# Attention's layernorm statistics of x in head slot 5 instead of head slot 7

## What is computed

```
_layernorm(x) = (x - mean(x)) / sqrt(var(x) + 1e-5)
x = x + tanh(g_xattn[0]) * xattn(_layernorm(x), ctx_1024, Wq, Wk, Wv, Wo, bo)
x = x + tanh(g_ffn[0])  * ffn(_layernorm(x), router_w, w_gate, w_up, w_down, ws_gate, ws_up, ws_down)
```

## Time and profile before

| what | before |
|---|---|
| median of 3 runs | 1902.89 us (1900.71 to 1904.76) |
| the profiled execution | 1910.31 us, its span 1908.6 us |
| mean granted TensorE clock | 0.987 of full speed |
| TensorE (PE) busy | 1842.6 us, 97% |
| VectorE (DVE) busy | 1452.8 us, 76% |
| ScalarE (ACT) busy | 960.2 us, 50% |
| GpSimd (POOL) busy | 811.3 us, 43% |
| SyncE's DMAs | 216864 packets, 205.86 MB |

### The profile page before, as it was taken

One profiled execution on the slowest core, in us unless ns is written; L12 is line 12 of the kernel. 1 busy time (PEld: TensorE's weight loads), 2 busy tenths in 40 slices (PEclk: granted clock), 3 DMA queues, 4 the chain that ended last, 5 costly groups with the idle time before them and its releaser, 6 DMA issues.

```text
span 1908.6 us, 32817 instructions
## 1 busy us (share of the span) xinstructions
PE 1842.6 (97%) x11280; PEld 1556.7 (82%) x11280; DVE 1452.8 (76%) x3217; ACT 960.2 (50%) x2260; POOL 811.3 (43%) x1067
## 2 busy tenths in 40 slices
PE   6999999999997899999999999999999999999999
PEld 5889988998896778888878888877888887888887
DVE  5788888888775777777887777787777778867776
ACT  4777877787776643334443433353434334433332
POOL 3445555555445443424624343353333443333330
PEclk9999999999997899999999999999999999999999
DMA  7888898998886332121132212114122112311111
GB/s 219 172 189 191 190 197 191 201 207 190 193 197 160 84 112 84 45 78 45 55 115 73 66 56 76 46 40 149 47 75 78 47 54 71 118 44 67 45 45 45
DMA packets 217029, 207.96 MB, mean 109 GB/s; under 512 B 113824, under 2 KB 169120, under 8 KB 216864
## 3 DMA queue, kind: packets, MB, share of 16 engines
q1 hardware_dynamic: 216864, 205.86, 42.3%
HBM read 111.43 MB, written 18.87 MB: 68 GB/s over the span
## 4 chain that ended last, share of the span: by engine, by line
PE 74%; DVE 13%; issue 5%; POOL 3%; ACT 2%; DMA 1%; SPq 1%; DVEq 0%; POOLq 0%; ACTq 0%
PE gate_up L1297 31%; PE down L1811 18%; PE bank L797 16%; PE scores L900 2%; DVE ops_lo L1154 2%; DVE acc L1662 2%; PE probs_t L931 2%; POOL hidden L1510 1%; PE rows_t L787 1%; DVE x_in L651 1%; DVE probs L729 1%; PE y L924 1%; PE down L1790 1%; PE y L922 1%; ACT probs L607 1%
## 5 line engine op out<-in xcount | busy, mean ns | idle before, releaser
L1297 PE MATMUL gate_up<-xo_hi,ops_hi 128*128 128x512 f32 x1120 | 440.5, 393 | 13.4 <-DVE hidden L1273 4.5
L1297 PE MATMUL gate_up<-xo_hi,ops_lo 128*128 128x512 f32 x1120 | 436.6, 390 | 0.0
L1297 PE MATMUL gate_up<-xo_lo,ops_hi 128*128 128x512 f32 x1120 | 436.4, 390 | 0.0
L607 ACT ACTIVATE probs<-probs,neg_max 128x128 f32<-128x128 f32 (+1 forms) x512 | 229.3, 450 | 108.2 <-DVE neg_max L729 106.5
L1662 DVE SCALAR_TENSOR_TENSOR acc<-down,scale,acc 128x512 f32<-128x512 f32 x320 | 239.0, 748 | 35.1 <-PE down L1811 34.7
L1297 PEld LDWEIGHTS gate_up<-xo_hi,ops_hi 128*128 128x128 f32 x1120 | 210.6, 188 | 67.5 <-DVE gated L1273 9.6
L1811 PE MATMUL down<-d_hi,h_hi 128*128 128x512 f32 x640 | 249.0, 389 | 0.0
L1811 PE MATMUL down<-d_lo,h_hi 128*128 128x512 f32 x640 | 249.0, 389 | 0.0
L1811 PE MATMUL down<-d_hi,h_lo 128*128 128x512 f32 x640 | 249.0, 389 | 0.0
L1297 PEld LDWEIGHTS gate_up<-xo_lo,ops_hi 128*128 128x128 f32 x1120 | 210.5, 188 | 44.4
L1297 PEld LDWEIGHTS gate_up<-xo_hi,ops_lo 128*128 128x128 f32 x1120 | 210.6, 188 | 42.3
(11 more groups left out here) (183 smaller groups left out, 4423.3 us busy)
## 6 DMA issues: line engine op xcount, KB each, us to landing
g_raw<-in_w_gate SPq DMA_DIRECT2D x40, 512.0 KB, 3.8
u_raw<-in_w_up SPq DMA_DIRECT2D x40, 512.0 KB, 3.8
d_raw<-in_w_down SPq DMA_DIRECT2D x40, 512.0 KB, 3.7
k_stack<-k_hi SPq DMA_DIRECT2D x128, 128.0 KB, 2.5
q_stack<-q_hi SPq DMA_DIRECT2D x128, 128.0 KB, 2.5
c_in<-in_ctx_t SPq DMA_DIRECT2D x16, 512.0 KB, 4.4
x_in<-in_x SPq DMA_DIRECT2D x16, 512.0 KB, 5.3
k_stack<-k_lo SPq DMA_DIRECT2D x64, 128.0 KB, 2.6
```

The costliest lines, as they stand in the source:

```text
L607: ins = act.activation(p, p, ACT.Exp, bias=neg_max[:, s, t:t + 1], scale=-1.0, accum_out=row_sum[:, s, t:t + 1])
L1297: ins = pe.matmul(gu_ps[bank][:], ops[x][:, which, a, c, :], xo[y][:, b, c, :], start=(begins and c == 0 and i == 0), stop=(c == CH - 1 an ...
```

## The change

`LN_SLOT` is 5 and no longer 7. Both uses of the constant follow: VectorE's `statistics(ln)` and GpSimd's `inverse_std(ln)`. `X_LOAD`, `XN_SLOT` and all other numbers stay.

```
-    LN_SLOT, C_SLOT, XN_SLOT = 7, 12, 10
+    LN_SLOT, C_SLOT, XN_SLOT = 5, 12, 10
```

## The result

The changed kernel takes 1928.89 us in the median of 4 runs (1927.08 to 1934.21), the kernel before on the same chip 1901.8 us (1900.49 to 1904.76). The ratio is 1.0149, 95% interval 1.0131 to 1.0167: slower by 27 us. The profiled execution took 1934.21 us, its span 1932.5 us, at the same mean granted clock of 0.987 as before; against the profiled execution of before that is +23.9 us. The forecast was 1916 us with a range to 1927 us: the direction came true, the size did not.

What follows compares the result with a forecast made beforehand. The prediction took TensorE to bound attention, with SyncE's in-order queue the tightest resource beside it. Terms 0 + 1 + 13.0 + 0 - 0.9 = +13 us on 1903 us gave 1916 us, range 1902 to 1927 us.

Steps and rivals of the forecast that it cites:

- VectorE in a plain batch: Statistics in slot 5 delay slot 6's maximum, but TensorE needs it 2 us later; slot 10's wait swallows any gain: 0.
- The load of x_in: Landing 0.3 us before the statistics' new place, at slowest 0.8 us late: +1 us, bounds 0 and +6.
- It compounds: Rival, chance 0.10: late queue delays x1's store, x_res, then x_in and the statistics; 14 us more, 1930 us.
- GpSimd's order and the standstill: Newton and the additions precede head 6's split, so SyncE's queue stands still 3.1 us before head 6's turn.
- The load of hat rows: On SyncE's queue, 1.8 us later per batch; VectorE waits 2.6 us; net +13.0 us, bounds +5 and +21, or 0.
- The queue absorbs it: Rival, chance 0.24: gaps and long issues behind the standstill take most of it up; 1905 or 1907 us.
- The turned halves: Head 10's turn issues up to 3 us later, possibly late for TensorE's next batch: 0, bounds 0 and +4.
- The start: TensorE's 0.86 us wait for the first batch's second q_lo vanishes: -0.9 us, bounds -0.9 and 0.
- Faster: Rival, chance 0.06: time leaving slot 7 removes TensorE's slot 12 wait for t_lo, saving 9 us: 1894 us.

Runs made afterwards that it cites:

- e3: The changed kernel with SyncE's load of x_res issued in slot 4, behind the load of x_in, instead of slot 2: 1920.88 us, ratio 1.0072.
- e1: The changed kernel with GpSimd's Newton operations back in slot 7, VectorE's statistics staying in slot 5: 1930.68 us, ratio 1.0119.
- e2: The changed kernel with GpSimd's two additions to x_res in slot 8 instead of 6: 1907.71 us, against 1906.75 us for the kernel before.
- e8: The changed kernel with the statistics and Newton operations in slot 6 instead of 5, on both engines: 1944.59 us.
- e4: The changed kernel with the load of hat rows issued in slot 10 instead of 14: 1934.48 us.
- e7: The changed kernel with GpSimd's additions to x_res in slot 8 and the load of x_res in slot 4: 1901.18 us, ratio 0.9993.

## Why the prediction was wrong in size

**VectorE in a plain batch, 0.** Right for the changed kernel: with x_in on time (e3) the plain batches cost +1.1 us over five. But the cover that I named, TensorE's late need for slot 8, was not the whole of it. It also needs GpSimd to be idle beside the statistics. Where it is not (e1), the same move costs 23 us in slots 12 and 13, falls of the clock included. I had checked who waits for the group, not who runs beside it.

**The load of x_in, +1, bounds 0 and +6.** This is the step that failed. The waits grew by 16.5 - 6.2 = 10.3 us, and moving x_res behind x_in (e3) takes back some 15 us by the ratios, 10.7 us by the slots. I priced the load from its issue time of before, 305.90 us, and let only its landing vary. But the issue time itself moves: the queue that the same change makes late carries it. The rival *It compounds* had this chain link by link, with a chance of 0.10 and 14 us. e3 bears out its mechanism and its size, but not its place: it saw the price in the hat batches, and of the 10.7 us that e3 takes back in the slots 8.0 us lie in the five plain ones, and the waits begin in batch 2, before the first hat row. What I set against it, that TensorE is late too and gives the load its time back, does not prevent the loss: eight batches have such a wait, and only 1, 5, 7, 9 and 10 have none. A second part of the 10 us stands in no term of the sum, a fall of the clock behind a wait of 1.85 us in batch 12, which costs 1.5 us in slot 13.

**GpSimd's order and the standstill, 3.1 us.** Right: 2.75 us in batch 7, 4.5 us where x_in was late (136.57 us against the end of the issue before at 132.03 us, in batch 2). e2 shows it as the cause of both prices.

**The load of hat rows, net +13.0.** Mechanism right, size low: slots 2 and 4 cost +17.2 us. Two terms were off. The wait rose to 23.5 / 8 = 2.94 us a batch where I had 2.6, since the gaps behind the standstill gave nothing back. And of it TensorE paid more than I allowed: 17.1 us in the hat batches on top of the 1.9 us of before (the forecast had 1.8 us), 19.0 of 23.5 us, so 0.56 us a batch were free and not 0.75. Besides slot 4 a second place begins to pay, slot 2, where t_lo stands behind the moments; in the kernel before slot 2 took 2.64 to 2.65 us in every batch, whatever the wait. *The queue absorbs it*, which had 0.24, is out by the same rows: the way behind the turn kept its 17.05 us. Its condition, that the long issues vanish while the queue stands still, did not come true either: between 80 and 560 us there are 31 in the trace of before and 31 in that of the changed kernel.

**The turned halves, 0.** TensorE's waits for them rose from 8.4 to 9.9 us, 1.5 us, inside the bound of +4.

**The start, -0.9.** Right: -1.3 us until slot 0 of batch 1.

***Faster*, 0.06.** Its mechanism was real in part, and my ground against it was wrong. I held that VectorE has caught up in slot 10, so nothing arrives in slot 12. But a VectorE that comes to the pair L651 0.08 us earlier is through both halves before head 10's split can take hold between them: in batches 5, 7, 9 and 10 of the changed kernel slot 12 is 2.4 us and not 3.2 us. Over all batches the pair takes 3.9 us less than before, which batches with a late x_in overspent.

The sum, from the slots: hat rows +17.2; x_in +3.3 in slots 7 and 8, +5.8 of lateness in slot 12 and +1.5 from the clock, together +10.6; the shorter pairs -3.9; other slots +2.2. That is +26.1 us in batches 1 to 13, and with -1.3, -1.2 and +0.4 us outside them +24.0 us, against +23.9 us between the profiled executions and +27.1 us between the medians. The forecast had +13 for the first term, +1 for the second, and neither the third nor the fourth.

The Trainium skill's rule on refills of instructions ("Runtime: NRT & Kernel Launch", section "Instruction fetch mechanics"), which the prediction weighed and called mostly hidden, has rows after all. The transfers of the profile's instruction queue go with SyncE's long issues (248 of 294, as counted above). In batch 7 of the changed kernel the two turns beside such a transfer took 0.9 and 1.1 us longer than the usual 1.25 us. If the refill is the cause, which was not tested, it is not hidden on this queue.

**Not settled.** Four more kernels gave no result: the kernel before profiled again; the changed kernel with one Newton step in place of three (the dose of GpSimd's work between the splits); the changed kernel with both loads moved together; and the kernel before with L651 in slot 11. So how the loss grows with what stands between the splits rests on two points (e2 and the changed kernel) and on e8. That slot 12 follows the pair and its start is a rule that fits all ten traces, not the result of moving L651 alone.

## What to carry to other kernels

When a group moves to an earlier place on one engine, read what the engine that consumes it puts between two hand-overs to an in-order queue; whatever is needed soonest behind the queue pays for that distance, and moving one load forward moved the bill here (e4) and did not pay it. Price a load from the issue time that it will have, not from the one it had, above all where the load before it in the queue waits for a store of the same late chain. And look at what the neighbour engine runs beside the moved group: the same eight VectorE instructions cost nothing next to an idle GpSimd and 0.93 us more next to its additions. And look at the granted clock, batch by batch: in e1 a wait of 1.75 us was followed by 3.41 us at half the clock, and batches with such a fall lost 3.0 us where the others lost 0.9 us, while the mean clock of the execution only went from 0.987 to 0.982.

## What the runs showed of the hardware

VectorE and GpSimd hold each other up whole instructions at a time. It hits some VectorE forms only. While GpSimd's long operations ran, L638 and L640 (128x2, SBUF to SBUF) went from 0.17 to as much as 1.3 us, L686 (two operands in SBUF) from 0.42 to between 0.57 and 1.27 us, and each L651 from 0.54 to between 0.9 and 1.4 us. In the same situation BATCH_NORM_STATS2 kept its 0.69 us, the row maxima their 0.29 and 0.42 us, t_lo and q_lo (one operand in PSUM) their 0.69 us, and the 128x1 steps L708 to L714 their 0.15 us. The one that starts first wins, by the records if it leads by 0.14 us or more: in e7 L651's second half has that lead and GpSimd's split grows, from 0.92 to 1.17 us; with a lead of 0.05 to 0.06 us, as in the kernel before, L651 is the one held. The Trainium skill has a rule for this in "SBUF — State Buffer", section "SBUF: two separate sides": the two share a port pair as an exclusive lock, held for a whole instruction by whichever starts first, and of VectorE's operations those in a two-port mode or with two operands in SBUF take part. The trace agrees on L686, and on the order but for the lead of 0.06 us just named; which mode L638, L640 and L651 run in, no row says.

TensorE's clock was granted at one of two levels, 2.4 and 1.2 GHz. In batch 7 of e1 it fell to the lower one 0.7 us after TensorE had gone back to work from a wait of 1.75 us, and in batch 12 of the changed kernel 1.5 us after a wait of 1.85 us; a product of 128x512 then took 0.63 us in place of 0.40 us.

I had not expected that so small an instruction could cost 1.2 us, nor that one slot of TensorE would take 2.42, 3.24 or 3.96 us according to which of two engines is some tenths of a microsecond earlier. Nor that one constant that moves 2.5 us of GpSimd's additions two slots would cost the kernel before 16 us and cure the changed kernel of 27.
